# Reordering a stored q, k, v record by head channel: pieces in the store instead of in the load

## The reference

```python
q = layernorm(x) @ Wq.T + bq;  k = ctx @ Wk.T + bk;  v = ctx @ Wv.T + bv
# each reshaped to [tokens, 16 heads, 16 channels]; attention is within one token, head by head
logits = einsum('bsid,bsjd->bsij', q, k) / 4;  attn = softmax(logits, -1)
out = einsum('bsij,bsjd->bsid', attn, v)      # then transposed so that heads come before tokens
x = x + out.transpose(0, 2, 1, 3).reshape(B, -1, 256) @ Wd.T + bd
# then layernorm, top-1 routing over 8 experts (256 -> 512 -> gelu -> 256), times the gate, plus x
```

## Time and profile before

| | us |
|---|---|
| median of 3 runs | 374.71 |
| lowest and highest | 372.6, 374.93 |
| the profiled execution | 373.31 |
| its span on the core | 371.5 |

### The profile page before, as it was taken

One profiled execution on the slowest core, in us unless ns is written; L12 is line 12 of the kernel. 1 busy time (PEld: TensorE's weight loads), 2 busy tenths in 40 slices (PEclk: granted clock), 3 DMA queues, 4 the chain that ended last, 5 costly groups with the idle time before them and its releaser, 6 DMA issues.

```text
span 371.5 us, 11173 instructions
## 1 busy us (share of the span) xinstructions
PE 338.2 (91%) x3755; PEld 289.7 (78%) x3755; DVE 259.8 (70%) x723; ACT 193.5 (52%) x525; POOL 284.4 (77%) x538
## 2 busy tenths in 40 slices
PE   7898699999999998896877897799999999999994
PEld 6686588888887877675655786689999999999993
DVE  6555778888888876888767456784656566666662
ACT  1002658877767784767776427413353535353431
POOL 3669769999989977867888377663777778888874
PEclk9999899999999999899699899998999999999999
DMA  6699979999999989998799012310222222222210
GB/s 229 221 278 297 253 178 250 245 263 273 250 283 268 262 227 285 303 285 215 202 370 372 19 59 82 95 59 29 66 68 72 69 60 73 65 69 74 64 46 1
DMA packets 55415, 63.87 MB, mean 172 GB/s; under 512 B 36558, under 2 KB 45919, under 8 KB 55360
## 3 DMA queue, kind: packets, MB, share of 16 engines
q1 hardware_dynamic: 50832, 52.77, 49.4%
q0 software_dynamic: 3744, 9.53, 8.7%
q10 hardware_dynamic: 784, 0.87, 0.7%
HBM read 42.00 MB, written 22.07 MB: 172 GB/s over the span
## 4 chain that ended last, share of the span: by engine, by line
PE 62%; DMA 13%; DVE 10%; issue 5%; POOL 4%; SPq 3%; ACT 1%; DVEq 1%; POOLq 0%; ACTq 0%
PE bQ L1139 16%; PE bKV L1109 8%; PE bL L1109 8%; PE bKV L941 5%; PE bKV L944 5%; PE bQ L1034 5%; DMA qkv_scr<-qkv 4%; PE bY L997 4%; DMA w<-in_W 4%; PE bO L964 3%; PE bL L953 3%; PE bT L1121 2%; DMA r<-in_xc 2%; PE bA L1046 2%; DMA wA<-in_wkvT 2%
## 5 line engine op out<-in xcount | busy, mean ns | idle before, releaser
L1139 PE MATMUL bQ<-w,wA 128*128 x312 | 74.9, 383 | 5.4 <-DVE r L791 3.4
L1139 PEld LDWEIGHTS bQ<-w,wA 128*128 128x128 f32 x312 | 56.7, 192 | 12.6 <-issue 6.5
L394 POOL TENSOR_TENSOR x<-ql,mask 128x1024 f32<-128x1024 f32 x32 | 60.6, 1892 | 2.2
L425 POOL DMA_INDIRECT out<-r,isc x39 | 41.0, 1052 | 16.7 <-issue 13.4
L837 ACT ACTIVATE pad<-ql 64x512 f32<-64x512 f32 x64 | 40.1, 626 | 23.5 <-DMA ql<-qkv_scr 23.1
L448 POOL DMA_INDIRECT r<-row_scr,ig x39 | 40.8, 1047 | 6.1 <-issue 2.9
L1109 PEld LDWEIGHTS bKV<-wA,r 128*128 128x128 f32 x320 | 38.5, 192 | 4.2 <-issue 2.4
L1109 PE MATMUL bKV<-wA,r 128*128 128x128 f32 x320 | 39.4, 276 | 2.4 <-DVE wA L778 2.4
L904 ACT ACTIVATE wA<-bL,r 128x128 f32<-128x128 f32 x76 | 21.6, 368 | 38.0 <-PE bL L1109 38.0
L904 ACT ACTIVATE wA<-bKV,r 128x128 f32<-128x128 f32 x80 | 22.8, 367 | 34.0 <-PE bKV L1109 34.0
L769 DVE TENSOR_SCALAR r<-w1b 128x1028 f32 x39 | 28.6, 732 | 15.5 <-issue 13.1
(11 more groups left out here) (175 smaller groups left out, 664.1 us busy)
## 6 DMA issues: line engine op xcount, KB each, us to landing
qkv_scr<-qkv SPq DMA_DIRECT2D x16, 768.0 KB, 6.1
ql<-qkv_scr SPq DMA_DIRECT2D x32, 384.0 KB, 5.7
r<-in_xc SPq DMA_DIRECT2D x15, 512.0 KB, 6.6
row_scr<-cat SPq DMA_DIRECT2D x32, 133.5 KB, 5.8
w1b<-in_W1b SPq DMA_DIRECT2D x8, 514.0 KB, 6.8
w<-in_W SPq DMA_DIRECT2D x8, 512.0 KB
xt<-in_x SPq DMA_DIRECT2D x15, 256.0 KB, 6.1
b2b<-in_b SPq DMA_DIRECT2D x4, 256.0 KB
```

Source lines behind the costliest of these rows:

```text
L394: eng.tensor_tensor(quarter(kx[:, z % 2, :]), spread(ql[z // 2 % 2][:, :, z % 2, 0:HD]), mask_k, ALU.mult).then_inc(S["kx"], 1)
L425: eng.indirect_dma_start(out, bass.IndirectOffsetOnAxis(ap=isc[k][:, :], axis=0), yo[k], None, bounds_check=NTOK - 1, oob_is_err=False).th ...
L1139: i_ = eng.matmul(bQ[:, 0:C], hT[b % 2][:, k, :], w2[:, bass.ds(eb * (KH * C) + k * C, C)], start=(k == 0), stop=(k == KH - 1))
```

## The change

The scratch gets the order of the load: for each pair, half, head channel, then the 64 tokens of the half, then the 96 values. The store writes it in two transfers, one for each half of the tokens; every partition's 16 groups of 384 bytes go to 16 places. The load is one transfer of 128 partitions, each of which reads 6,144 contiguous bytes. The counts on the semaphores follow: a store now gives 32, a load 16. What the record holds, on either side, is the same as before.

```diff
-    qkv_scr = nc.dram_tensor("qkv_scr", [NT // 2, P, NH, 2, W3], f32, kind="Internal").ap()
+    qkv_scr = nc.dram_tensor("qkv_scr", [NT // 2, 2, NH, NC_ * NG_, 2 * W3], f32, kind="Internal").ap()
...
-                    eng.dma_start(qkv_scr[p], qkv[p % 2][:, :, :, :]).then_inc(S[f"st_q{p % 2}"], 16)
+                    for h in range(2):
+                        eng.dma_start(qkv_scr[p][h].rearrange("x n w -> n x w"),
+                                      qkv[p % 2][64 * h:64 * (h + 1), :, :, :].rearrange("p x w d -> p x (w d)")
+                                      ).then_inc(S[f"st_q{p % 2}"], 16)
...
-                    eng.wait_ge(S[f"st_q{p % 2}"], (p // 2 + 1) * 16)
+                    eng.wait_ge(S[f"st_q{p % 2}"], (p // 2 + 1) * 32)
...
-                    for h in range(2):
-                        eng.dma_start(ql[p % 2][64 * h:64 * (h + 1), :, :, :],
-                                      qkv_scr[p].rearrange("(h c g) x w d -> h x c g (w d)", h=2, c=NC_)[h]
-                                      ).then_inc(S[f"ld_q{p % 2}"], 16)
+                    eng.dma_start(ql[p % 2][:, :, :, :].rearrange("p g w d -> p (g w d)"),
+                                  qkv_scr[p].rearrange("h x (c n) w -> (h x c) (n w)", c=NC_)
+                                  ).then_inc(S[f"ld_q{p % 2}"], 16)
```

More of the change, by code:

```diff
@@ L385, in pool_attention @@
                         eng.wait_ge(S["mask4"], 1)
-                    eng.wait_ge(S[f"ld_q{z // 2 % 2}"], (z // 4 + 1) * 32)
+                    eng.wait_ge(S[f"ld_q{z // 2 % 2}"], (z // 4 + 1) * 16)
                     if z > 1:
@@ L548, in vector_kv @@
             if a > 3:
-                eng.wait_ge(S[f"st_q{a // 2 % 2}"], a // 4 * 16)
+                eng.wait_ge(S[f"st_q{a // 2 % 2}"], a // 4 * 32)
             eng.tensor_tensor(record(a)[:, 0:3:2, :, :], bKV[:, :].rearrange("p (w x c) -> p w x c", w=2, c=HD),
```

## The result

| | kernel before | changed kernel |
|---|---|---|
| median of 13 runs each | 373.99 us | 379.55 us |
| lowest and highest | 372.08, 375.1 | 375.36, 384.83 |
| profiled execution (span) | 373.31 (371.5) | 379.52 (377.7) |

The changed kernel takes 1.012 times as long, 95% interval 1.009 to 1.015: slower by 1.2%, some 5 us, where a gain of 4.4 us was forecast.

A forecast was written before the change was run, and what follows sets the result against it. A DMA chain of record load, x, row and store slightly longer than PE's pair was taken to bound attention. Gains 0.57 + 1.91 + 1.94 = 4.4 us gave 368.9 profiled, 370.3 as median; range 366.5 to 394.

The forecast's parts named there:

- What bounds the kernel: Attention part: the DMA chain load, x, row, store, landing, next load is slightly longer than PE's pair (9.86 us).
- L': Transfer time of the new contiguous record load: 1.9 us at 412 GB/s, 2.1 us less than the old load's 4.0.
- X: Transfer time of the new store in small pieces: 3.7 us, bounds 1.9 to 8.0; the old store takes 1.9.
- d: Change in the DMA chain's length per cycle, new load and store against old: -0.3 us, adding up to 2.4 over eight cycles.
- the gain of 1.91: Two tiles made late by xc, at 134 and 145.7 us, return to 4.93 us each: 0.46 + 1.45 us.
- SP and xc, costed at nothing: SP's issue sum stays; the second store issue delays xc's issue 0.6 to 1.2 us, but xc waits behind store data anyway.
- Order of landing: x, behind the load and before the store, lands 2.1 us earlier; the late x at 110 us goes, gaining 0.57.
- The 1.94 us before the down product: PE's idle time before the first down product goes, since the expert matrices land some 5 us earlier.
- The signs it named: If right: small packets unchanged, load landing some 4.1 us, store at most 8, load issues at most 10 apart, named waits gone.
- the dear writes: Rival at every store: small written pieces cost more than read ones, X = 6.0, +22.5 us, 397 us; chance 0.30.
- the cost only changes sides: Rival: store grows by what the load saves, gain 2.5, 372.2 us; chance 0.25 together with compute absorbing the gain.
- The bound that the prediction drew from it: If 64 partitions get half bandwidth, the split store's transfer could not be under 3.8 us; the gain still holds.

The follow-up runs named there:

- e2: Kernel before, with the context load (xc) issued ahead of the record's store for all pairs: 389.10 us, ratio 1.044.
- e16: Kernel before, with the x load issued behind the xc load, in the gap between store and load, for all pairs: 369.47 us, ratio 0.987.
- e4: Changed kernel with the two old loads in small pieces brought back, store kept in small pieces (attention values misplaced): 395.05 us, ratio 1.054.
- e5: Changed kernel with the xc load ahead of the record's store for the first four pairs only: 377.20 us, ratio 1.008.
- e15: Kernel before with its store split into two transfers of 64 partitions, pieces still 6,144 B: 380.63 us, ratio 1.017.
- e3: Changed kernel storing and loading the record whole in 6,144 B pieces, not reordered (attention values misplaced): 369.45 us, ratio 0.987.
- e8: Kernel before with one whole store in small pieces and two loads of 64 partitions in 6,144 B pieces: 382.21 us, ratio 1.023.
- e18: Changed kernel with the x load issued just ahead of the record's load, both after the store has landed: ratio 1.011.
- e7: Changed kernel with 1,024 B of padding behind each head channel's block in the scratch: 379.01 us, ratio 1.013.

## Why the prediction was wrong

*What bounds the kernel* held. The chain was right in its members: e2 puts 1.27 us into it and loses 15.0, e16 takes 0.64 out, wins some 5, and ends the wait of 3.9 us that the prediction read.

*The load* was mis-sized. L' was set to 1.9 us by the row of 412 GB/s, which shows stores and matrices in full stream. e4 gives 2.75 (4.0 - 1.25): the first 16 packets of the contiguous load take 1.5 to 6 times the 234 ns of the later ones. The saving is some 1.25 us a cycle, not 2.1.

*The store* was right within its bounds in the chain: X = 3.7 was forecast and 3.2 measured, give or take 0.4. With both, d = X - 1.9 + L' - 4.0 is near zero (+0.1) instead of -0.3, as the cycles of 10.42 and 10.33 have it, and the gain of 1.91 that hung on it fell away. But X is not one number: on the empty queue the store takes 5.2 us instead of 2.9.

*SP and xc, costed at nothing: the step that failed.* "xc waits behind the store's data anyway" took for granted a chain in steady state. Three things were left out. At the start the chain has not yet formed: the first store has nothing queued ahead, PE already waits for tile 6's xc in the kernel before (1.53 us at 31.41, a row that the prediction did not look for), and what the store is longer falls on PE: its start is 2.6 us late at tile 6. The lower clock that came after the wait made it 1.5 us more, by the lengths of the two matmul groups. e5 shows the step (xc ahead of the store at the start, and the 3.4 us at tile 8 are gone), and e15 shows that the store's split alone is enough for it (+3.5). And in later pairs xc does not get the load's saving, as the prediction had it: its landing grew from 6.3 to 7.7 us, behind a store that takes 7.4 instead of 5.3. That this, with the later x, is the second loss of 2.3 us is the likely reading and not shown by a run of its own. The cover that was named for the extra store issue was no cover there.

*Order of landing.* x was to land 2.1 us earlier whatever X is, and to win 0.57. The x issued behind the load at 64.28 landed at 71.0, against 66.3 behind the load at 58.71 before: 4.7 later with the tiles 3.4 late, so 1.3 later, and its waits grew.

*The 1.94 us before the down product* went, as said, but not by earlier matrices: the last one landed at 208.0 instead of 204.16, and PE came 6.8 us later. The first down product, timeline of PE:

```profile
212.17 1.99 PE L1141 MATMUL bQ<-w,wA 128*128 x8 [0.38 <-ACT wA L906]
```

*The signs it named.* Right: packets under 512 B unchanged. At its limit: a store half landed in 8.0 us before 112, and that store as a whole in 8.6. Wrong, and listed as such: load issues not within 10 us, load landing 6.0 instead of 4.1, more waits on xc and x, a lower clock. *The rivals.* The time came out on the side of the dear writes, but not by that mechanism: X was not 6.0, and a written piece of 384 B took 22 ns by the median, less than a read one (27). That the range up to 394 holds 379.55 is luck: its upper part was drawn for this rival. In the chain the nearest case was that the cost only changes sides (X = 4.0, d = 0), which would have given 372.2; the start, which no rival named, and the later landings of xc and x put it on the slower side.

*The two rules.* The half rate of 64 partitions, left undecided by the rows of before, is now shown for a transfer alone on the queue: 197 against 418 GB/s with nothing else changed. By the Trainium skill, SBUF — State Buffer, section Door 1: The DMA port swizzle, a transfer of partitions 0 to 63 reaches half the ports; the trace agrees. The bound that the prediction drew from it (X not under 3.8 us) did not hold in the chain, where X is 3.2 and other transfers run beside the store. The Trainium skill, DMA: Bandwidth & Descriptors, section Specifications, gives 512 B as the least size for full rate, with a read-modify-write below it. That the rate falls agrees: the whole store in 384 B pieces moved 242 to 262 GB/s against 418. That this costs written pieces an extra read and read ones nothing was the prediction's own reading, and the times of 22 and 27 ns speak against it; whether a read-modify-write takes place no run here shows.

## What to carry to other kernels

When a store grows, look at what is issued right behind it on the same queue, and price it twice: once in the steady chain, and once in the first iterations, where the queue is nearly empty and nothing hides it. Find the terms that stand between a store's landing and the next one; here one us in that chain was worth some 10, and moving a load of 0.64 us out of it into the gap between store and load won as much as large pieces on both sides would have (e16 and e3, 0.987 each). Splitting a store in two halves of 64 partitions halved its rate on an empty queue.

## What was not expected of the hardware

- xc's issue (L257) takes SP 0.43 us by the median, 1.91 at most, in the kernel before, but 1.9 to 4.65 us behind a store of 2,048 small pieces; behind halves in large pieces (e15) it was 0.58 to 2.52.
- A written 384 B piece is cheap: its packets take 22 ns by the median (mean 25.6), the read pieces of the kernel before 27 (mean 33.5).
- A contiguous load of 128 x 6,144 B does not start as a store of the same shape: its packets take 353 ns on average, most of the excess over 234 in the first 32. Not caused by fresh data, pitch or tensor; placing x ahead of it takes 30 ns off (323), and xc out of its way 50 (302).
- A transfer 2.5 us late cost 4.1 us by tile 6: after PE's wait of 1.99 us the granted clock was 0.50 for 3 us. The length of the wait alone does not decide it: the waits of 1.77 us in e8 and 2.74 in e18 were followed by no such fall between 33 and 42 us. In e18, with the same store, the lag at tile 8 was 1.4 us instead of 3.4. e7 had the fall earlier, after tile 4's wait of 2.20 us (0.52 from 26 to 28 and 0.51 to 29.5), and a lag of 4.1.
